# The opening of a fused adapter and expert-FFN kernel: expert split without the identity in it, up bias by PE, residuals by DVE, the first xT in token halves

## The reference

```python
# layer 0: adapter, one of 16 experts per batch, chosen by domain_id
hidden = gelu(x @ down_W.T + down_b)                 # 512 -> 128
expert_out = hidden @ expert_W[idx].T + expert_b[idx]
hidden = where(valid, expert_out, hidden) + domain_emb[idx]
x1 = layernorm(hidden @ up_W.T + up_b + x, eps=1e-5) * ln_gamma + ln_beta   # 128 -> 512
# layer 1: FFN, one of 8 experts per batch
h = gelu(x1 @ Wi[e] + bi[e])                         # 512 -> 2048
y = layernorm(h @ Wo[e] + bo[e] + x1, eps=1e-12) * gamma[e] + beta[e]
```

## Time and profile before

| | us |
|---|---|
| time, median of 3 runs (781.38 to 781.60) | 781.49 |
| time of the profiled execution | 781.23 |
| its span, first to last instruction | 779.4 |
| PE busy in the span | 762.1 |
| DVE, POOL, ACT busy | 516.7, 466.2, 347.4 |

### The profile page before, as it was taken

The page is one execution under the profiler, slowest core; times in us unless marked ns, Lnnn a source line. Parts: engine busy times, 40 slices in busy tenths (PEclk is TensorE's granted clock), DMA queues, the critical chain, the costliest instruction groups (busy, mean ns, idle before and its releaser), DMA issues.

```text
span 779.4 us, 10642 instructions
## 1 busy us (share of the span) xinstructions
PE 762.1 (98%) x3418; PEld 631.0 (81%) x3418; DVE 516.7 (66%) x1064; ACT 347.4 (45%) x601; POOL 466.2 (60%) x401
## 2 busy tenths in 40 slices
PE   8999999999999999999999999999999999999996
PEld 7878887888878888788887888878887888888885
DVE  6676874678556894578837798277874778646115
ACT  3454445434445344534445444444445434443432
POOL 5766654675647756386644855548654676646444
PEclk9999999999999999999999999999999999999999
DMA  9930000310012000137212200022000110001001
GB/s 325 407 126 1 1 0 1 122 41 0 1 56 82 27 1 1 70 115 276 81 55 68 95 0 1 3 95 68 1 1 1 64 45 1 0 12 43 1 0 54
DMA packets 17049, 45.70 MB, mean 59 GB/s; under 512 B 2274, under 2 KB 2530, under 8 KB 16098
## 3 DMA queue, kind: packets, MB, share of 16 engines
q1 hardware_dynamic: 16274, 43.67, 15.4%
q10 hardware_dynamic: 720, 1.31, 0.6%
HBM read 36.59 MB, written 8.39 MB: 58 GB/s over the span
## 4 chain that ended last, share of the span: by engine, by line
PE 91%; DVE 4%; issue 2%; ACT 1%; DMA 1%; POOL 0%; ACTq 0%; DVEq 0%; POOLq 0%
PE acc L751 15%; PE acc L753 15%; PE acc L752 14%; PE ps_h L751 14%; PE ps_h L753 14%; PE ps_h L752 14%; PE ps L751 2%; PE ps L753 2%; PE ps L752 2%; DVE xt L525 1%; DVE rows L607 1%; DMA xt_raw<-in_xT 1%; ACT ps_h L434 1%; PE ps_h L823 0%; DVE x1t L590 0%
## 5 line engine op out<-in xcount | busy, mean ns | idle before, releaser
L274 POOL TENSOR_TENSOR wi<-w_raw,wi 128x512 fp32r<-128x512 f32 x128 | 165.4, 1293 | 257.0 <-ACT wi L418 256.9
L433 ACT ACTIVATE h<-ps_h,bi_now 128x512 fp32r<-128x512 f32 x126 | 86.9, 690 | 372.3 <-PE ps_h L753 372.2
L595 DVE TENSOR_TENSOR h<-ps_h,h 128x512 fp32r<-128x512 f32 x126 | 87.0, 691 | 198.5 <-ACT ps_h L434 197.6
L751 PE MATMUL acc<-wo,h 128*128 128x512 f32 x512 | 199.2, 389 | 0.0
L752 PE MATMUL acc<-wo,h 128*128 128x512 f32 x512 | 199.2, 389 | 0.0
L753 PE MATMUL acc<-wo,h 128*128 128x512 f32 x512 | 199.2, 389 | 0.0
L751 PE MATMUL ps_h<-x1t,wi 128*128 128x512 f32 (+1 forms) x512 | 197.7, 386 | 0.4 <-DVE x1t L590 0.2
L752 PE MATMUL ps_h<-x1t,wi 128*128 128x512 f32 (+1 forms) x512 | 197.5, 386 | 0.0
L753 PE MATMUL ps_h<-x1t,wi 128*128 128x512 f32 (+1 forms) x512 | 197.5, 386 | 0.0
L280 POOL TENSOR_TENSOR wo<-w_raw,wo 128x512 fp32r<-128x512 f32 x128 | 165.9, 1297 | 7.1 <-ACT wo L424 7.1
L584 DVE STREAM_TRANSPOSE ps<-rows 32x128 f32<-32x128 f32 x448 | 144.2, 322 | 5.7
(11 more groups left out here) (129 smaller groups left out, 584.6 us busy)
## 6 DMA issues: line engine op xcount, KB each, us to landing
w_raw<-in_w SPq DMA_DIRECT2D x32, 512.0 KB, 8.5
rows<-in_x SPq DMA_DIRECT2D x32, 256.0 KB, 2.8
out<-rows SPq DMA_DIRECT2D x32, 256.0 KB, 2.0
xt_raw<-in_xT SPq DMA_DIRECT2D x7, 1024.0 KB, 4.8
vec<-in_vec SPq DMA_DIRECT2D x2, 768.0 KB, 10.7
xt_raw<-in_xT ACTq DMA_DIRECT2D x4, 256.0 KB, 6.1
vec<-in_vec SPq DMA_DIRECT2D x1, 512.0 KB, 6.6
down_raw<-in_down ACTq DMA_DIRECT2D x1, 256.5 KB, 2.7
```

The lines of the kernel that those rows point to most:

```text
L274: pool.tensor_tensor(slot[:, 1], w_raw[:, c, 0, :].rearrange("p (k i) -> p k i", k=KD), slot[:, 0].bitcast(F32), ALU.subtract).then_inc(wi ...
L433: act.activation(h[:, c % H_RING, 0, :], bank, ACT.Gelu, bias=bias)
L595: dve.tensor_tensor(h[:, c % H_RING, 1, :], hidden_bank(t, c), h[:, c % H_RING, 0, :].bitcast(F32), ALU.subtract).then_inc(h_split, 1)
L751: pe.matmul(out, left[0], right[0], start=start, stop=False)
```

## The change

- **Up bias.** up_b arrives as one row of 2 KB. PE starts each of the four accumulators with a float32 product of a column of ones (one partition) and that row (first_up_bias), ahead of adapter_down. bias_product then adds to them. POOL's four add_up_bias of the first tile are gone; DVE's first_sum adds the unchanged row blocks. The broadcast up_b is loaded later, for the later tiles.
- **Expert matrix.** It is split without the identity: expert_round on ACT (scale by validity, hi), expert_rest on DVE (lo). The scaled identity exp_off is a fifth operand: fold_product has five matmuls in place of three. Validity is computed by POOL. The down bias comes as a column of the expert load. The expert bias of batch 0 is made by three ACT instructions.
- **Down weights.** Their lo part is made by DVE.
- **xT.** The four pieces are two feature groups by 256 tokens: pieces 0 and 1 hold the first half of the tokens. first_down(0) and (1), then the first half of the hidden, fold_w, and adapter_up of blocks 0 and 1 come ahead of first_down(2) and (3). ACT makes up_W's hi part ahead of the pieces.
- **Rows.** Block 0 is normalized alone, then block 1, with the sum of block 1 and the second hidden rest in between.
- **Warm-up.** Six warm-up products at the start in place of 14; the others are gone.
- **POOL.** wi_rest(0, 0) comes after the first inverse root, wi_rest of chunks 1 to 3 after the second; add_out_bias moves into steps 1 to 4 of the first tile.
- **Tile 0.** The first two pieces of the second tile's xT are split ahead of the gelus and not in step 0. The first tile's gelus read bi directly and DVE's copy of it is gone. SP waits once for all four row blocks before it loads the next ones.

first_stats, first_var, first_center and first_scale hold normalize's instructions for one block; first_rest and first_hid_rest are xt_rest and hid_rest for a piece and a half.

```diff
-WARM = (14, 1, 12, 6)
+WARM = 6
...
-down_raw = sb("down_raw", [P, D + 1])
+down_raw = sb("down_raw", [P, D])
...
-exp_raw = sb("exp_raw", [P, BATCH, A + 2])
-exp_off = down_raw[:, 0:A]
+exp_raw = sb("exp_raw", [P, BATCH, A + 3])
+down_b = exp_raw[:, 0, A + 2:A + 3]
+exp_off = [fold_w[:, b, 1, 0:A] for b in range(BATCH)]
...
+up_b_row = up_b[0:1, 0, :]
+ones = rows[0:1, 1, 1, 0:P]
...
+def fold_bank(b):
+    return ps0[:, 1, :] if b else ps_h[:, 0, :]
...
+def half(j):
+    return slice(j // 2 * HALF, (j // 2 + 1) * HALF)
...
+def pair(j):
+    return slice(j % 2 * 2, j % 2 * 2 + 2)
...
+    sp.dma_start(up_b_row, vec0_d[0, 0:1, :]).then_inc(up_b_row_landed, 16)
...
-        if s == 0:
-            sp.dma_start(up_b[:, 1:2, :], vec0_d[:, 0:1, :].to_broadcast([P, 1, D])).then_inc(up_b_landed, 16)
...
+    sp.dma_start(up_b[:, 1:2, :], vec0_d[:, 0:1, :].to_broadcast([P, 1, D])).then_inc(up_b_landed, 16)
...
+    sp.wait_ge(xb_ready, SUB)
...
-        sp.wait_ge(xb_ready, s + 1)
...
-    pool.wait_ge(down_w_hi, 1)
-    pool.tensor_tensor(down_w[:, 1, :, :], down_raw[:, 0:D].rearrange("p (k i) -> p k i", k=KD),
-                       down_w[:, 0, :, :].bitcast(F32), ALU.subtract).then_inc(down_w_ready, 1)
-    pool.wait_ge(valid_ready, 1)
-    pool.wait_ge(down_w_ready, 1)
-    step(pool.tensor_scalar(exp_off[:, :], ident[:, :], valid[:, 1, 0:1], None, ALU.mult))
-    pool.wait_ge(exp_landed[0], 16)
-    w = exp_raw[:, 0, 0:A]
-    step(pool.tensor_scalar(w, w, valid[:, 0, 0:1], None, ALU.mult))
-    step(pool.tensor_tensor(w, w, exp_off[:, :], ALU.add))
-    step(pool.tensor_copy(exp_w[:, 0, :], w))
-    pool.tensor_tensor(exp_w[:, 1, :], w, exp_w[:, 0, :].bitcast(F32), ALU.subtract).then_inc(exp_w_ready, 1)
...
-    pool.wait_ge(up_b_landed, 16)
-    for s in range(SUB):
-        add_up_bias(0, 1, s, 0)
+    pool.wait_ge(ids_all_landed, 16)
+    step(pool.tensor_scalar(valid[:, 0, :], ids_all[:, :], 0.0, None, ALU.is_ge))
+    step(pool.tensor_scalar(valid[:, 1, :], ids_all[:, :], float(E0), None, ALU.is_lt))
+    step(pool.tensor_tensor(valid[:, 0, :], valid[:, 0, :], valid[:, 1, :], ALU.mult))
+    step(pool.tensor_scalar(valid[:, 1, :], valid[:, 0, :], -1.0, 1.0, ALU.mult, ALU.add))
+    pool.sem_inc(valid_ready, 1)
+    pool.tensor_scalar(exp_off[0], ident[:, :], valid[:, 1, 0:1], None, ALU.mult).then_inc(exp_off_ready, 1)
...
+    wi_rest(0, 0)
...
-    wi_rest(0, 0)
...
+    wi_rest(0, 2)
+    wi_rest(0, 3)
...
-    wi_rest(0, 2)
-    wi_rest(0, 3)
...
-    for s in range(SUB):
-        add_out_bias(0, 0, s, 0)
...
-            if c in (1, 2, 3, 4) and not (isinstance(t, int) and t == 0):
-                inverse_root(1, t - 1, c - 1)
+            if c in (1, 2, 3, 4):
+                if isinstance(t, int) and t == 0:
+                    add_out_bias(0, 0, c - 1, 0)
+                else:
+                    inverse_root(1, t - 1, c - 1)
...
-    for k in range(KD):
-        act.dma_start(xt_raw[:, k, :], xT_d[0, :, k, :]).then_inc(xt_first[k], 16)
+    for j in range(KD):
+        act.dma_start(xt_raw[:, pair(j), half(j)], xT_d[0, :, pair(j), half(j)]).then_inc(xt_first[j], 16)
...
+    def first_round(j):
+        act.wait_ge(xt_first[j], 16)
+        act.activation(x1t[1][:, 0, pair(j), half(j)], xt_raw[:, pair(j), half(j)], ACT.Copy).then_inc(xt_hi, 1)
...
+    def first_hidden(j, done):
+        act.wait_ge(down_done, j + 2)
+        act.activation(hid[:, 0, half(j)], ps0[:, j // 2, half(j)], ACT.Gelu, bias=down_b)
+        act.activation(ps0[:, j // 2, half(j)], ps0[:, j // 2, half(j)], ACT.Gelu,
+                       bias=down_b).then_inc(done, 1)
...
-    for k in range(KD):
-        xt_round(0, k)
+    def expert_round():
+        act.wait_ge(valid_ready, 1)
+        act.wait_ge(exp_landed[0], 16)
+        act.activation(exp_w[:, 0, :], exp_raw[:, 0, 0:A], ACT.Identity,
+                       scale=valid[:, 0, 0:1]).then_inc(exp_hi, 1)
...
+    def first_expert_bias():
+        act.activation(hid_b[:, :], exp_raw[:, 0, A:A + 1], ACT.Identity, scale=valid[:, 0, 0:1],
+                       bias=exp_raw[:, 0, A + 1:A + 2]).then_inc(act_step, 1)
+        act.wait_ge(act_step, 1)
+        act.activation(exp_b[:, 0, :], hid_b[:, :].to_broadcast([P, P]), ACT.Copy).then_inc(act_step, 1)
+        act.wait_ge(act_step, 2)
+        act.activation(exp_b[:, 1, :], exp_b[:, 0, :].bitcast(F32), ACT.Identity, scale=-1.0,
+                       bias=hid_b[:, :]).then_inc(exp_b_ready, 1)
...
-    act.wait_ge(down_landed, 16)
-    hidden(0)
+    first_round(0)
+    first_round(1)
+    expert_round()
+    first_round(2)
+    first_round(3)
+    first_expert_bias()
+    first_hidden(0, half_hi)
...
+    first_hidden(2, hid_hi)
...
+    wi_round(0, 0, 2)
...
-    for c in range(2, WI_AHEAD):
-        wi_round(0, 0, c)
+    wi_round(0, 0, 3)
...
+    xt_round(1, 0)
+    xt_round(1, 1)
...
-            if more and c in (0, 1):
+            if more and c in (0, 1) and not (isinstance(t, int) and t == 0 and c == 0):
...
+    def first_rest(j):
+        dve.wait_ge(xt_hi, j + 1)
+        part = x1t[1][:, :, pair(j), half(j)]
+        dve.tensor_tensor(part[:, 1], xt_raw[:, pair(j), half(j)], part[:, 0].bitcast(F32),
+                          ALU.subtract).then_inc(xt_split, 1)
...
+    def expert_rest(b):
+        dve.scalar_tensor_tensor(out=exp_w[:, 1, :], in0=exp_raw[:, b, 0:A], scalar=valid[:, 0, b:b + 1],
+                                 in1=exp_w[:, 0, :].bitcast(F32), op0=ALU.mult,
+                                 op1=ALU.subtract).then_inc(exp_w_ready, 1)
...
-    dve.wait_ge(ids_all_landed, 16)
-    step(dve.tensor_scalar(valid[:, 0, :], ids_all[:, :], 0.0, None, ALU.is_ge))
-    step(dve.tensor_scalar(valid[:, 1, :], ids_all[:, :], float(E0), None, ALU.is_lt))
-    step(dve.tensor_tensor(valid[:, 0, :], valid[:, 0, :], valid[:, 1, :], ALU.mult))
-    dve.tensor_scalar(valid[:, 1, :], valid[:, 0, :], -1.0, 1.0, ALU.mult, ALU.add).then_inc(valid_ready, 1)
...
-    dve.tensor_copy(down_w[:, 0, :, :], chunks(down_raw[:, 0:D])).then_inc(down_w_hi, 1)
-    for k in range(KD):
-        xt_rest(0, k)
+    step(dve.tensor_copy(down_w[:, 0, :, :], chunks(down_raw[:, :])))
+    dve.tensor_tensor(down_w[:, 1, :, :], chunks(down_raw[:, :]), down_w[:, 0, :, :].bitcast(F32),
+                      ALU.subtract).then_inc(down_w_ready, 1)
...
-    dve.wait_ge(valid_ready, 1)
-    expert_bias(0)
-    hid_rest(0)
+    first_rest(0)
+    first_rest(1)
+    dve.wait_ge(exp_hi, 1)
+    expert_rest(0)
+    first_rest(2)
+    first_rest(3)
+    first_hid_rest(0, half_hi, half_split)
...
-    adapter_sum(0, 0, 0, acc_part(0))
-    adapter_sum(0, 1, 0, acc_part(1))
+    def first_sum(s):
+        dve.wait_ge(up_done, s + 1)
+        dve.wait_ge(rows_landed[s], 16)
+        dve.sem_inc(xb_ready, 1)
+        dve.tensor_tensor(acc[:, s, :], acc[:, s, :], rows[:, 0, s, :], ALU.add).then_inc(sum_ready[0], 1)
...
+    first_sum(0)
+    first_stats(0)
+    first_var(0)
...
-    adapter_rows(0, (0, 1), 0, acc_part)
-    adapter_sum(0, 2, 0, acc_part(2))
+    first_center(0)
+    first_sum(1)
+    first_scale(0)
+    first_stats(1)
+    first_var(1)
+    first_center(1)
+    first_hid_rest(2, hid_hi, hid_split)
+    first_scale(1)
+    first_sum(2)
...
-    adapter_sum(0, 3, 0, acc_part(3))
+    first_sum(3)
...
+    xt_rest(1, 0)
+    xt_rest(1, 1)
...
-            if more and c in (0, 1):
+            if more and c in (0, 1) and not (isinstance(t, int) and t == 0 and c == 0):
...
+    def first_down(j):
+        pe.wait_ge(xt_split, j + 1)
+        for k in (j % 2 * 2, j % 2 * 2 + 1):
+            last = three(ps0[:, j // 2, half(j)], [down_w[:, i, k, :] for i in (0, 1)],
+                         [x1t[1][:, i, k, half(j)] for i in (0, 1)], k == 0, k == KD - 1)
+        last.then_inc(down_done, 1)
...
+        pe.wait_ge(exp_off_ready, b + 1)
...
-        three(ps0[:, 1, :], [exp_w[:, i, :] for i in (0, 1)], [up_w[:, i, :] for i in (0, 1)],
-              True, True).then_inc(fold_done, 1)
+        three(fold_bank(b), [exp_w[:, i, :] for i in (0, 1)], [up_w[:, i, :] for i in (0, 1)], True, False)
+        pe.matmul(fold_bank(b), exp_off[b], up_w[:, 0, :], start=False, stop=False)
+        pe.matmul(fold_bank(b), exp_off[b], up_w[:, 1, :], start=False, stop=True).then_inc(fold_done, 1)
...
+    def first_up_bias(s):
+        pe.matmul(acc[:, s, :], ones, up_b_row, start=True, stop=False)
...
-        pe.wait_ge(hid_split, u + 1)
+        if isinstance(u, int) and u == 0 and s < 2:
+            pe.wait_ge(half_split, 1)
+        else:
+            pe.wait_ge(hid_split, u + 1)
...
-    pe.wait_ge(const_ready, 3)
-    keep_warm(WARM[0], ps_h[:, 1, :])
...
+    pe.wait_ge(const_ready, 4)
+    keep_warm(WARM, ps_h[:, 1, :])
+    pe.wait_ge(up_b_row_landed, 16)
+    for s in range(SUB):
+        first_up_bias(s)
...
-    for k in range(KD):
-        adapter_down(0, k)
-    keep_warm(WARM[1], ps_h[:, 1, :])
+    first_down(0)
+    first_down(1)
...
```

(52 more changed lines are left out.)

52 lines of the change are left out of this document (31 added, 21 removed).

## The result

The changed kernel takes 783.94 us (median of 22 runs, 780.52 to 785.11) beside 781.57 of the kernel before (22 runs, 780.85 to 782.22): ratio 1.0026, 95% interval 1.0019 to 1.0034. It is slower by 2.4 us, where 2.4 us less was forecast; the difference is small (0.3%), and the interval leaves out 1. Its profiled execution took 783.96 us, with a span of 782.1, 2.7 more than before.

A forecast was written before the change was run, and what follows sets the result against it. PE was taken as the bound, without a break from about 44 us and waiting on other engines before. Gains of 1.9 and 1.0 less 0.45 made 2.4 us, so a median of 779.1 us, with a range of 778.0 to 781.8.

The forecast's parts named there:

- First step: Opening, ACT's chain from expert matrix to fold: first adapter_up starts at 14.2 in place of 14.98, 0.8 us earlier.
- rival 3: Opening loads: smaller packets delay xT and the expert by 1.8 us, giving 780.9 us; chance 0.08.
- The up bias on PE: Opening: eight bias instructions, four at low and four at high clock, end by 9.7 and cost nothing.
- the prediction's own signs of being wrong: first_down waiting for bias products, matmuls behind 20 us at twice the pitch, or new POOL or DVE waits in steps 1-4.
- rival 2: Opening: PE's clock stays low through the fold, adapter_up 3.8 us late and 0.7 longer, 783.6 us; chance 0.10.
- Second step: DVE's chain to the second row block: 6.7 us serially, FFN starts at 24.05, 0.3 us earlier than 24.35.
- Third step: Early FFN products: POOL's 1.42 us wait for wi goes, second half starts at 31.15, not 33.05; 1.9 us gained.
- Fourth step: Hole near 44 us at the second tile's xT split shrinks from 1.14 to 0.23 us; 1.0 us gained.
- Fifth step: fold_product(1) has two more matmuls of 0.23 us where PE is full: 0.45 us lost, at most 2.
- The sum: Whole kernel: 1.9 + 1.0 - 0.45 = 2.4 us gained; profiled execution 778.8 us, median 779.1.
- Rival 4: DVE's longer chain eats the first step; FFN starts as late as before or 0.6 us later, 780.1 us; chance 0.10.
- Rival 1: Opening: PE's clock rises only near 11 us, adapter_up starts at 15.45, 1.25 us later, 780.4 us; chance 0.17.

The follow-up runs named there:

- e2: Changed kernel without the four bias products (first tile lacks the up bias) and with 14 warm-up products, not six; 779.94 us, ratio 0.9979 to the kernel before.
- e1: Changed kernel with the bias products over 128 rows, 127 of them zero, in place of one; 780.59 us, ratio 0.9987 to the kernel before.
- e3: Changed kernel with 14 warm-up products in place of six, one-row bias products kept; 782.99 us, ratio 1.0011 to the kernel before.
- e6: e4 with the first two xT pieces of the second tile split in step 0 again, as before the change; 780.26 us, ratio 0.9982.
- e4: Changed kernel with POOL adding the first tile's up bias, no bias products on PE, 14 warm-up products; 778.60 us, ratio 0.9966 to the kernel before.
- e9: e4 with 20 warm-up products in place of 14; 778.44 us, ratio 0.9962 to the kernel before.

## Why the prediction was wrong

- **First step**: right but for the clock. The expert landed at 9.25 (forecast 9.4 to 9.7 for its round), the three bias instructions on ACT took 1.1 (1.0), and without the products adapter_up came at 13.69 (14.2). Smaller packets cost nothing: rival 3 is out.
- **The up bias on PE: the step that failed.** It was priced at nothing, four products at the low and four at the high level, ended by 9.7, "with cover of 1 us". All eight ran low and ended at 12.2; first_down started right behind, at 12.15, 2.85 after it did without them (e2): the first of the prediction's own signs of being wrong. Its twelve matmuls and the first four of fold_product ran low too, and adapter_up came at 18.36. The text chose "above the full price, which I take" for one row of contraction. The price of the instruction was right, 0.45 at the high level and 0.90 at the low. (The Trainium skill, TensorE: Matmul & The Clock Gate, "Why this matters for your kernels", says that few rows take as long as a full matmul. The trace agrees: at the low level the starts are 0.85 us apart with one row and with e1's 128.) What the step took for granted is that the level rises during them as before. That it does not was rival 2, with 0.10: adapter_up at 18.0 and 783.6 us; measured 18.36 and 783.94. In part the close time is luck: rival 2 had 0.7 us for a slower adapter_up, which ran high, and did not have the 1.07 of the loop's returns. The argument for it was in the text (no row shows the level rise during products of one row), the one against it (no gap longer than 1.42) was about gaps, and e3 shows a fall with no gap. "Nothing" fails for full rows as well: of the 4.27 us by which the second half is late on the forecast, the one row makes 2.64 (35.42 against e1's 32.78), and 1.63 stay with full rows (32.78 against 31.15) in e1's profile, the slowest of its eleven runs; its median is 0.96 lower, which would leave about 0.7 (an estimate). Behind the 1.63 are a bias row that came late (5.79 in e1, 5.03 in the changed kernel, 4.4 forecast) and a level that rose after 10 us and not at 7.9.
- **Second step**: DVE's chain took 6.41 from the first sum to the end of the second scale (19.51 to 25.92), 6.7 forecast. From adapter_up to the second half 17.06, forecast 16.95.
- **Third step**: POOL's wait of 1.42 is gone, and the early chunks run unbroken from 28.40. Held.
- **Fourth step**: -1.13 (1.0). Held; e6 shows it by itself.
- **Fifth step**: +0.45. Held; none of its wider bound of 2 came about, PE has no gap there.
- **The sum** missed by 783.96 - 778.8 = 5.2: 4.27 from the second half (35.42 against 31.15) and 1.07 from the loop's returns, which no step named, less 0.13 of the fourth step.
- Rival 4 is out: the first step's gain arrived in e4 (FFN at 23.77). Rival 1, a late rise after a short warm-up, a wait for the bias row and products of one row, is not what the changed kernel did. It is close to what e1 did, with full rows: the level rose after 10 us, adapter_up came at 15.74 (15.45 in rival 1) and the median is 780.59 (780.4).

Open: the runs of the changed kernel reach from 780.5 to 785.1, 4.6 us apart over 22 runs, where e9's five lie within 0.5. The mean granted clock of each run gives a hint. The six fastest (780.52 to 783.14) and one more (783.62) have 0.992 to 0.994, the other fifteen (783.58 to 785.11) 0.997 to 0.999. The faster runs with the lower mean fit a level that rose early, was recorded, and fell again, as in e3's profile (0.993); in the changed kernel's profile (783.96, 0.997) the low opening is not counted, since the column shows 1.00 there. No profile of one of the seven was taken, so this is not shown.
